# Attention norms of a six-layer transformer kernel: squares of both halves added on GpSimd, norm matmuls halved and moved

## The chip, the cores and the metric

The kernel runs on one core of one Trainium2 chip. The metric is the device time of one execution in microseconds (us). A core has engines that run side by side, each with its own queue in program order: PE (TensorE, matmuls), PEld (its weight loads), DVE (VectorE), ACT (ScalarE), POOL (GpSimd) and SP, which here only issues DMAs. Semaphores order the engines among each other.

## What is computed

A batch of 16 sequences of 256 tokens and 128 channels goes through an adaptive layer norm, a small normalised attention, and then six layers of local attention (16 heads of 64, windows of 32) with a gated feed-forward block. In each layer the queries and keys are normalised per head before the rotary turn:

```
def l2norm(t):
    return t / jnp.maximum(jnp.linalg.norm(t, axis=-1, keepdims=True), 1e-12)
...
qkv = x @ Wqkv
q, k, v = (sh(q), sh(k), sh(v))
q = l2norm(q) * qs
k = l2norm(k) * ksc
q = q * cos * scale + rotate_half(q) * sin * scale
k = k * cos * inv + rotate_half(k) * sin * inv
out = local_attention(q, k, v)
```

## The kernel before, in words

After a first part (about 165 us) the kernel walks 96 batches of work: 6 layers times 16 sequences. Each engine has an order written out by hand as a table of step names (`PE_ORDER`, `DVE_ORDER`, `ACT_ORDER`, `POOL_ORDER`, `SP_ORDER`, from line 50), and the function `walk` goes through that table once a **period**. Steps named in `AHEAD` work already on the next batch, those in `BEHIND` still on the one before, so one period holds parts of three batches. There is no scheduler: an engine runs its steps in the order of its table, and waits where a semaphore isn't there yet.

The steps that matter here; digits are the head couple p (0, 1 for k; 2, 3 for q), a token tile or a half:

- PE: `PAp`, `PBp` project the first and second halves of the head dimensions of couple p into a PSUM bank (line 1229); `NK`, `NQ` sum squares over a head with matmuls against 0/1 columns, 32 columns wide, for k and q (line 1240, eight matmuls of 256 columns, two halves into four groups of 32 rows of `small_ps`); `TK`, `TQ` transpose the clamped sums (1248); `TU` transposes the inverse k norms (1255), `KN` spreads them over the head dimensions (1264); `V0` to `V3` project values (1274); `S` are the scores (1284, 1292), `T` transpose probabilities (1303), `PV` multiply with values (1321), `WO` is the output projection (1331); `CEN` and `VAR` make the feed-forward layer norm's centring and variance (1345, 1349), `UP` and `DN` its matmuls (1360, 1367).
- DVE: `RA`, `RB` multiply a projection bank with the rotary tables (988); `CK`, `CQ` clamp the sums of squares (1016); `UC` copies the transposed inverse norms (997), `KM` scales k with them (1004); `TC` copies transposed probabilities (1033), `M` is the row maximum (1021), `XA` adds the residual into `xs1` in two instructions (1054, 1055), `XB` again into `x1` (1059), `XG` scales by the standard deviation (1064), `H` is gate times value (1071), `X` ends the layer (1076), `AR` is the reciprocal of the softmax sums (1040).
- ACT: `QA`, `QB` square a projection bank into `square` (725); `E` are the softmax exponentials, 16 heads in four parts (769); `SQ`, `LN` belong to the layer norm (777, 782, 786); `LG` and `LE` load function tables (750, 752); `G` is the gelu (793); `RTK`, `RTQ` turn sums of squares into inverse norms (742, 747); `VC` copies values, `OC` attention outputs.
- POOL: `AD` adds the two rotary products (612), `AN` scales probabilities by inverse sums (597), `RK` splits inverse k norms into three bf16 parts (583 to 591), `TB` makes the tables of the next layer, once a layer.

Before, the squares of the two halves lie in four `square` buffers; `QA2` waits until `NK` has read the k squares (`norm_made`), and `NK` waits for all four squares. The chains to keep in mind: `WO` → `XA` → `CEN` → `SQ` → `VAR` → `LN` → `XG` → `UP`, and `TU` → `UC` → `KN` → `KM` → the key move by DMA → the next period's `S`.

```
PA0 PB0 PA1 S00 S01 PB1 BI WO PA2 NK CEN PB2 VAR PA3 PB3 TK UP0 UP1 S10 S11 V0 UP2 T00 TU NQ KN0 PAD V1 PV00 KN1
TQ T01 V2 DN T10 PV01 V3 T11 PV10 PV11
```

That is the order of PE before.

Of the kernel before, what the change touches and what calls it, by code (L numbers as in the profile page):

```python
# [9 lines left out]
ALU = mybir.AluOpType  # L10
# [3 lines left out]
P = 128  # L14
BATCH, TOKENS, DIM = 16, 256, 128
DEPTH, HEADS, DIM_HEAD, WINDOW = 6, 16, 64, 32
# [12 lines left out]
QUADS = HEADS // 4  # L29
COUPLES = QUADS // 2  # L30
QK_BANKS = 4 * COUPLES
# [16 lines left out]


PE_ORDER = """  # L50
PA0 PB0 PA1 S00 S01 PB1 BI WO PA2 NK CEN PB2 VAR PA3 PB3 TK UP0 UP1 S10 S11 V0 UP2 T00 TU NQ KN0 PAD V1 PV00 KN1
TQ T01 V2 DN T10 PV01 V3 T11 PV10 PV11
"""
DVE_ORDER = """
XS RA0 RB0 RA1 M0 RB1 BI XA XB AR00 RA2 RB2 CK XG RB3 RA3 H0 M1 AR01 H1 TC00 UC H2 KM0 CQ VC1 KM1 AR10 TC01 X
AR11 TC10 VC3 TC11
"""
ACT_ORDER = """
# [1 line left out]
RTQ OC11  # L60
"""
POOL_ORDER = """
AD0 AD1 AD2 AN00 AD3 TB RK AN01 AN10 AN11
"""
SP_ORDER = """
LK MQ MK LV LL MV
# [17 lines left out]
def steps_of(text):  # L84
# [8 lines left out]
PE_ORDER, DVE_ORDER, ACT_ORDER, POOL_ORDER, SP_ORDER = (  # L93
    steps_of(text) for text in (PE_ORDER, DVE_ORDER, ACT_ORDER, POOL_ORDER, SP_ORDER))
PE_FIRST, DVE_FIRST, ACT_FIRST, POOL_FIRST = (
    [(word.split(":")[0], int(word.split(":")[1])) for word in text.split()]
    for text in (PE_FIRST, DVE_FIRST, ACT_FIRST, POOL_FIRST))
FIRST_AHEAD = max(stage for _, stage in PE_FIRST + DVE_FIRST + ACT_FIRST + POOL_FIRST)
AHEAD = ("XS", "V", "VC", "PA", "PB", "RA", "RB", "QA", "QB", "AD", "NK", "NQ", "CK", "CQ", "TK", "TQ", "RTK", "RTQ",
         "RK", "TU", "UC", "KN", "KM", "LK", "LV", "MV", "MK", "MQ", "TB")  # L100
BEHIND = ("BI", "WO", "XA", "XB", "CEN", "SQ", "VAR", "LN", "XG", "UP", "G", "H", "DN", "X", "LF", "LG")


# [5 lines left out]
def rank(order, s, *kinds):  # L109

    return [x for x in order if x[0] in kinds].index(s)
# [7 lines left out]
def build(nc, t):  # L119

    with ExitStack() as ctx:
        def sb(name, shape, dt=F32):
            return ctx.enter_context(nc.sbuf_tensor(name, shape, dt))

        def sem(name):
            return ctx.enter_context(nc.semaphore(name))
# [6 lines left out]
        norm2_ps = small_ps[:, 0:TOKENS]  # L133
# [6 lines left out]
        head_ones = sb("head_ones", [P, WINDOW])  # L140
# [24 lines left out]
        prod = sb("prod", [P, 2, 2, 2, 2 * TOKENS])  # L165
        prod_a, prod_b = ([prod[:, i, a, :, :] for i in range(2)] for a in range(2))
        square = [[sb(f"square{i}_{a}", [P, 2 * TOKENS]) for a in range(2)] for i in range(COUPLES)]
        ks = sb("ks", [P, 2, QUADS, TOKENS])
        qs = sb("qs", [P, 2, QUADS, TOKENS])
        norm2 = sb("norm2", [P, TOKENS])  # L170
# [39 lines left out]
        def carve(parts, *shape):  # L210
# [15 lines left out]
            if len(shape) == 3:  # L226
# [82 lines left out]
         f_kg, f_y, f_gw, f_xb, f_x1) = (  # L309
            sem("f_" + n) for n in ("qkv sq eps inv q2 k2 v kcol max kmax log r qfin kv kvt qt qtc kw kg y gw xb x1").split())  # L310

        xs_ready, proj_ready, prod_ready, sq_ready, rot_ready, v_made, v_even_ready, v_odd_ready = (
            sem(n) for n in ("xs_ready", "proj_ready", "prod_ready", "sq_ready", "rot_ready", "v_made",
                             "v_even_ready", "v_odd_ready"))
        norm_made, clamped, norm_turned, norms_ready, rk_parts, rk_turned, rkt_ready, kn_made, kn_ready = (
            sem(n) for n in ("norm_made", "clamped", "norm_turned", "norms_ready", "rk_parts", "rk_turned",
                             "rkt_ready", "kn_made", "kn_ready"))
# [16 lines left out]
        def at(g, per_batch, n=0):  # L334

            return g * per_batch + (CREDIT + n)

        def start_with_credit(eng, *sems):
            for s in sems:
                eng.sem_inc(s, CREDIT)  # L340
# [185 lines left out]

        @block.gpsimd
        def _(pool):
            start_with_credit(pool, scaled, rk_parts, rot_ready, f_gw, f_xb)
            pool.memset(xs[:, :], 0.0)  # L530
            pool.memset(xs1[:, :], 0.0)
            pool.memset(mean_ones[:, :], 1.0 / DIM)
# [3 lines left out]
            def make_tables(layer):  # L536
                pool.wait_ge(scales_landed, layer * 16 + 16)
                for m in range(2):
                    for a in range(2):
                        col = qk_scales[:, 2 * m + a:2 * m + a + 1]  # L540
                        pool.tensor_scalar(tables[:, m, a, a, :], rotary[:, m, 0, :], col, None, ALU.mult)
                        last = pool.tensor_scalar(tables[:, m, a, 1 - a, :], rotary[:, m, 1, :], col,
                                                  -1.0 if a else 1.0, ALU.mult, ALU.mult)
                last.then_inc(tables_ready, 1)
# [7 lines left out]
            for i in range(TILES):  # L552
                for j in range(PAIRS):
                    last = pool.tensor_copy(mask_bf[:, i, j, :], mask[:, i, :])
# [21 lines left out]
            def step(s, g, b, parity, layer):  # L576
                kind = s[0]
                if kind == "RK":

                    pool.wait_ge(norms_ready, at(g, 2, 1))  # L580
                    pool.wait_ge(rk_turned, at(g, 1))
                    alone(pool)
                    pool.tensor_copy(rk_bf[:, :, 0, :], rk[:, :, :]).then_inc(rk_parts, 1)
                    pool.wait_ge(rk_parts, at(g, 4, 1))
                    pool.tensor_tensor(rk_rest[:, :, :], rk[:, :, :], rk_bf[:, :, 0, :], ALU.subtract
                                       ).then_inc(rk_parts, 1)
                    pool.wait_ge(rk_parts, at(g, 4, 2))
                    alone(pool)
                    pool.tensor_copy(rk_bf[:, :, 1, :], rk_rest[:, :, :]).then_inc(rk_parts, 1)
                    pool.wait_ge(rk_parts, at(g, 4, 3))  # L590
                    pool.tensor_tensor(rk_bf[:, :, 2, :], rk_rest[:, :, :], rk_bf[:, :, 1, :], ALU.subtract
                                       ).then_inc(rk_parts, 1)
                if kind == "AN":
                    i, c = s[1], s[2]
                    part = slice(4 * c, 4 * c + 4)
                    pool.wait_ge(inv_ready, at(g, 2 * TILES, 2 * i + c + 1))
                    pool.tensor_tensor(probs[i][:, part, :, :].rearrange("p j e k -> p (j e) k"),  # L597
                                       probs[i][:, part, :, :].rearrange("p j e k -> p (j e) k"),
                                       inv_sums[i][:, part, :].rearrange("p j (e o) -> p (j e) o", o=1)
                                       .to_broadcast([P, PAIRS, KEYS]), ALU.mult).then_inc(scaled, 1)  # L600
                if kind == "TB" and b == BATCH - 1 and layer < DEPTH - 1:
                    pool.wait_ge(prod_ready, at(g, QK_BANKS, QK_BANKS))
                    make_tables(layer + 1)
                if kind == "AD":
                    p = s[1]
                    n, c = p // COUPLES, p % COUPLES
                    last_product = max(rank(DVE_ORDER, (h, p), "RA", "RB") for h in ("RA", "RB"))
                    pool.wait_ge(prod_ready, at(g, QK_BANKS, last_product + 1))
                    if c == 0 and g > 0:
                        pool.wait_ge((k_moved, q_moved)[n], moved(g))  # L610
                    dst = (ks, qs)[n][:, :, 2 * c:2 * c + 2, :].rearrange("p a u c -> p a (u c)")
                    pool.tensor_tensor(dst, prod_a[p % 2], prod_b[p % 2], ALU.add  # L612
                                       ).then_inc(rot_ready, 1)
# [5 lines left out]
        def _(act):  # L619
# [98 lines left out]
            def step(s, g, b, parity, layer):  # L718
                kind = s[0]
                if kind in ("QA", "QB"):  # L720
                    p, a = s[1], int(kind == "QB")
                    n = p // COUPLES
                    act.wait_ge(prod_ready, at(g, QK_BANKS, rank(DVE_ORDER, ("RB" if a else "RA", p), "RA", "RB") + 1))
                    act.wait_ge(norm_made, at(g, 2, n))
                    nc.scalar.activation(square[p % COUPLES][a][:, :], bank_of(("PB" if a else "PA", p))[:, :],  # L725
                                         ACT.Square, bias=zero_col[:, :]).then_inc(sq_ready, 1)
                if kind == "VC":
# [25 lines left out]
                if kind == "OC":  # L753
                    i, c = s[1], s[2]
# [333 lines left out]
        def _(pe):  # L1088
# [129 lines left out]
            def step(s, g, b, parity, layer):  # L1218
# [12 lines left out]
                    last.then_inc(proj_ready, 1)  # L1231
                if kind in ("NK", "NQ"):
                    n = int(kind == "NQ")
                    last_square = max(rank(ACT_ORDER, (x, COUPLES * n + c), "QA", "QB")
                                      for x in ("QA", "QB") for c in range(COUPLES))
                    pe.wait_ge(sq_ready, at(g, QK_BANKS, last_square + 1))
                    pe.wait_ge(norms_ready, at(g, 2, n))
                    for a in range(2):
                        for u in range(QUADS):
                            last = mm(norm2_ps[WINDOW * u:WINDOW * (u + 1), :], head_ones[:, :],  # L1240
                                      square[u // 2][a][:, TOKENS * (u % 2):TOKENS * (u % 2 + 1)],
                                      start=(a == 0), stop=(a == 1), skip_group_check=True)
                    last.then_inc(norm_made, 1)
                if kind in ("TK", "TQ"):
                    n = int(kind == "TQ")
# [206 lines left out]
```

## Time and profile before

| what | value |
|---|---|
| runs | 3487.27, 3490.45, 3495.57 us; median 3490.45 us |
| profiled execution | span 3500.8 us from first to last instruction (the page gives no other time for it) |
| busy | PE 96%, PEld 71%, DVE 70%, ACT 77%, POOL 41% |
| PE clock granted | mean 0.982 of full speed |
| chain that ended last | PE 69%, POOL 18%, issue 4%, DVE 2% |

The page lists busy time per engine, the chain of work that ended last, and the costliest groups of instructions by line. A timeline lists instructions in order of time with start and length; for PE the ends are modelled, so the start of one step to the start of the next is the better length of a step.

### The profile page before, as it was taken

To read this page: it belongs to the slowest core of one execution; us is meant where nothing else is said; L and a number is where in the kernel's file an instruction comes from. 1 tells how busy PE (TensorE), PEld (TensorE's weight loads), DVE (VectorE), ACT (ScalarE), POOL (GpSimd) and SP (SyncE) were. 2 spreads that over 40 slices of the span, in tenths; PEclk is the share of its full clock that TensorE was granted. 3 is DMA by queue.
4 is the path that set the end of the run, shared out by engine and by line. 5 is a ranking of instruction groups with operands and counts; after the bars stand their busy time and mean duration, and the time that the engine had idled before them with its cause. 6 is when DMAs were issued, how large, how long until landed. Compare 5 with 4: busy or idle time off the path is not lost.

```text
span 3500.8 us, 152322 instructions
## 1 busy us (share of the span) xinstructions
PE 3344.2 (96%) x63036; PEld 2479.3 (71%) x63228; DVE 2441.7 (70%) x5141; ACT 2702.7 (77%) x9033; POOL 1445.3 (41%) x1276
## 2 busy tenths in 40 slices
PE   6789999999999999999999999999999999999997
PEld 4457777677777767777767777767767767777775
DVE  5667777667777767777767777767767767777774
ACT  5667787768778777878777887868778787878876
POOL 2244444434444443444444444444444353444441
PEclk9899999999999999999999999999999999999998
DMA  2055656555655656565565566555555655565563
GB/s 71 1 115 122 140 122 129 121 123 120 143 123 123 132 118 134 127 130 126 112 138 118 127 135 131 120 130 117 127 129 121 133 129 127 117 130 126 116 135 76
DMA packets 361273, 421.42 MB, mean 120 GB/s; under 512 B 52291, under 2 KB 265814, under 8 KB 359814
## 3 DMA queue, kind: packets, MB, share of 16 engines
q1 hardware_dynamic: 360582, 411.67, 54.4%
q8 instruction: 499, 8.18, 1.0%
q14 instruction: 192, 1.57, 0.1%
HBM read 19.30 MB, written 2.10 MB: 6 GB/s over the span
## 4 chain that ended last, share of the span: by engine, by line
PE 69%; POOL 18%; issue 4%; DVE 2%; DMA 1%; ACT 1%; SPq 0%; POOLq 0%; DVEq 0%
PE ring_ps L1229 16%; POOL qs L612 12%; PE out_ps L1321 12%; PE out_ps L1331 9%; PE ring_ps L1274 8%; PE small_ps L1240 6%; PE score_ps L1292 4%; PE ring_ps L1303 4%; PE ring_ps L1367 4%; POOL probs L597 3%; DVE prod L988 2%; PE ring_ps L1264 2%; PE out_ps L1345 2%; PE score_ps L1284 1%; PE small_ps L1248 1%
## 5 line engine op out<-in xcount | busy, mean ns | idle before, releaser
L769 ACT ACTIVATE probs<-score_ps,neg_max,rq 128x64 f32<-128x64 f32 x3072 | 1194.7, 420 | 97.0 <-DVE neg_max L1026 95.7
L988 DVE TENSOR_TENSOR prod<-ring_ps,tables 128x512 f32<-128x512 f32 x1536 | 957.9, 681 | 292.4 <-PE ring_ps L1229 264.8
L612 POOL TENSOR_TENSOR ks<-prod 128x1024 f32<-128x1024 f32 x192 | 452.9, 2359 | 870.9 <-DVE prod L988 870.9
L1229 PE MATMUL ring_ps<-xs,wqk 128*128 128x256 f32 x3072 | 771.2, 389 | 17.2 <-issue 11.9
L769 ACT ACTIVATION_READ_ACCUMULATOR probs<-score_ps,neg_max,rq 128x1 f32 x3072 | 677.4, 221 | 0.0
L725 ACT ACTIVATE square<-ring_ps,biases 128x512 f32<-128x512 f32 x768 | 516.9, 687 | 200.9 <-DVE prod L988 199.1
L597 POOL TENSOR_TENSOR probs<-probs,inv_sums 128x512 f32<-128x512 f32 x384 | 401.0, 1044 | 608.8 <-DVE inv_sums L1040 608.7
L1229 PEld LDWEIGHTS ring_ps<-xs,wqk 128*128 128x128 f32 x3072 | 572.9, 192 | 107.3 <-issue 18.9
L612 POOL TENSOR_TENSOR qs<-prod 128x1024 f32<-128x1024 f32 x192 | 453.4, 2361 | 395.1 <-DVE prod L988 395.1
L1321 PEld LDWEIGHTS out_ps<-pt,v 64*64 64x64 f32 x24576 | 399.5, 136 | 119.2 <-issue 117.0
L758 ACT ACTIVATE att_t<-out_ps 128x512 f32<-128x512 f32 x384 | 217.0, 591 | 312.1 <-PE out_ps L1321 311.5
L1321 PE MATMUL out_ps<-pt,v 64*64 64x32 f32 x24576 | 433.4, 221 | 9.5 <-issue 6.7
L1274 PE MATMUL ring_ps<-wv,xs 128*128 128x512 f32 x768 | 431.1, 644 | 0.7 <-ACT vs L731 0.7
L1331 PE MATMUL out_ps<-att_t,wo 128*128 128x256 f32 x1536 | 350.9, 381 | 1.9 <-ACT att_t L758 1.2
L1292 PEld LDWEIGHTS score_ps<-kt,qt 64*32 64x32 f32 x24576 | 264.5, 105 | 90.2 <-issue 82.4
L1331 PEld LDWEIGHTS out_ps<-att_t,wo 128*128 128x128 f32 x1536 | 292.5, 191 | 43.5 <-issue 2.2
L1033 DVE COPY pt<-ring_ps 128x512 f32<-128x512 f32 x384 | 259.6, 676 | 82.2 <-PE out_ps L1321 78.2
L1292 PE MATMUL score_ps<-kt,qt 64*32 64x64 f32 x24576 | 297.8, 226 | 6.1 <-issue 5.0
L1004 DVE TENSOR_TENSOR ks<-ks,ring_ps 128x512 f32<-128x512 f32 x384 | 246.7, 684 | 73.0 <-PE ring_ps L1264 72.6
L1360 PE MATMUL out_ps<-xg,w 128*128 128x256 f32 (+1 forms) x1152 | 283.8, 383 | 3.2 <-DVE xg L1064 3.2
L1021 DVE TENSOR_REDUCE row_max<-score_ps 128x8 f32<-128x512 f32 x384 | 246.4, 684 | 24.1 <-PE score_ps L1292 20.2
L1360 PEld LDWEIGHTS out_ps<-xg,w 128*128 128x128 f32 (+1 forms) x1152 | 199.3, 180 | 80.6 <-DVE hidden L1071 30.2
(182 smaller groups left out, 3809.4 us busy)
## 6 DMA issues: line engine op xcount, KB each, us to landing
v<-vs SPq DMA_DIRECT2D x1344, 128.0 KB
qt<-qs SPq DMA_DIRECT2D x768, 128.0 KB
kt<-ks SPq DMA_DIRECT2D x768, 128.0 KB
v<-vs SPq DMA_DIRECT2D x192, 64.0 KB
wqk<-in_L_ffn_Wqkv SPq DMA_DIRECT2D x6, 1024.0 KB, 5.2
wv<-in_L_ffn_Wqkv SPq DMA_DIRECT2D x6, 512.0 KB, 4.5
wo<-in_L_ffn_Wo SPq DMA_DIRECT2D x6, 512.0 KB
out_dram<-ks SPq DMA_DIRECT2D x16, 128.0 KB, 1.9
```

Of the source, the lines that this page charges most:

```text
L597: pool.tensor_tensor(probs[i][:, part, :, :].rearrange("p j e k -> p (j e) k"), probs[i][:, part, :, :].rearrange("p j e k -> p (j e) k"), ...
L612: pool.tensor_tensor(dst, prod_a[p % 2], prod_b[p % 2], ALU.add).then_inc(rot_ready, 1)
L725: nc.scalar.activation(square[p % COUPLES][a][:, :], bank_of(("PB" if a else "PA", p))[:, :], ACT.Square, bias=zero_col[:, :]).then_inc(sq ...
L769: last = nc.scalar.activation(probs[i][:, j, e, :], score_ps[e][:, KEYS * j:KEYS * (j + 1)], ACT.Exp, bias=neg_max[:, h:h + 1], scale=rq[p ...
L988: last = V.tensor_tensor((prod_b if a else prod_a)[p % 2][:, f, :] .rearrange("p (u c) -> p u c", u=2), bank[:, :].rearrange("p (u c) -> p ...
L1033: V.tensor_copy(pt[:, 4 * c:4 * c + 4, :], bank_of(("T", i, c))[:, :].rearrange("p (j c) -> p j c", c=P)).then_inc(t_copied, 1)
L1229: last = mm(bank_of(s)[:, TOKENS * f:TOKENS * (f + 1)], wqk[:, n, 2 * c + f, a, :], xs[:, WINDOW:PADDED], start=True, stop=True)
L1274: mm(bank_of(s)[:, :], xs[:, WINDOW + P * i:WINDOW + P * (i + 1)], heads[:, :, e, :], start=True, stop=True).then_inc(v_made, 1)
L1292: last = mm(score_ps[e][WINDOW * w:WINDOW * (w + 1), KEYS * j:KEYS * (j + 1)], qt[64 * e:64 * e + 64, j, q0:q0 + WINDOW], kt[64 * e:64 * e ...
L1321: last = mm(out_ps[j % 2][side:side + 64, q0:q0 + WINDOW], v2[64 * e:64 * e + 64, WPT * i + w, DIM_HEAD * j:DIM_HEAD * (j + 1)], pt[64 * e ...
L1331: last = mm(out_ps[0][:, 0:TOKENS], wo[layer % 2][:, j, :], att_t[:, j, :], start=(j == 0), stop=(j == PAIRS - 1))
L1360: last = mm(out_ps[c % 2][0:size, TOKENS * n:TOKENS * (n + 1)], w1[layer % 2][:, col:col + size], xg[:, :], start=True, stop=True)
```

## The change

GpSimd gets a new step `SS` for each head couple p: it adds the squares of the two halves (128x512) into a buffer of their own, `square_sum`. `NK` and `NQ` then read the sums, with four matmuls in place of eight. `QAp` and `QBp` wait for the sum of the couple that used the same `square` buffers before, in place of `norm_made`. `NK` moves behind `PB2`, `NQ` from before `KN0` to behind `V2`, `TQ` from before `T01` to behind `V3`, `CQ` on DVE from between `KM0` and `VC1` to behind `TC01`.

```
 PE_ORDER = """
-PA0 PB0 PA1 S00 S01 PB1 BI WO PA2 NK CEN PB2 VAR PA3 PB3 TK UP0 UP1 S10 S11 V0 UP2 T00 TU NQ KN0 PAD V1 PV00 KN1
-TQ T01 V2 DN T10 PV01 V3 T11 PV10 PV11
+PA0 PB0 PA1 S00 S01 PB1 BI WO PA2 CEN PB2 NK VAR PA3 PB3 TK UP0 UP1 S10 S11 V0 UP2 T00 TU KN0 PAD V1 PV00 KN1
+T01 V2 NQ DN T10 PV01 V3 TQ T11 PV10 PV11
 """
 DVE_ORDER = """
-XS RA0 RB0 RA1 M0 RB1 BI XA XB AR00 RA2 RB2 CK XG RB3 RA3 H0 M1 AR01 H1 TC00 UC H2 KM0 CQ VC1 KM1 AR10 TC01 X
+XS RA0 RB0 RA1 M0 RB1 BI XA XB AR00 RA2 RB2 CK XG RB3 RA3 H0 M1 AR01 H1 TC00 UC H2 KM0 VC1 KM1 AR10 TC01 CQ X
 AR11 TC10 VC3 TC11
 """
...
 POOL_ORDER = """
-AD0 AD1 AD2 AN00 AD3 TB RK AN01 AN10 AN11
+AD0 SS0 AD1 SS1 AD2 AN00 AD3 TB RK AN01 SS2 SS3 AN10 AN11
 """
...
+        square_sum = [sb(f"square_sum{i}", [P, 2 * TOKENS]) for i in range(COUPLES)]
...
+                if kind == "SS":
+                    p = s[1]
+                    n, c = p // COUPLES, p % COUPLES
+                    last_square = max(rank(ACT_ORDER, (x, p), "QA", "QB") for x in ("QA", "QB"))
+                    pool.wait_ge(sq_ready, at(g, QK_BANKS, last_square + 1))
+                    pool.wait_ge(norm_made, at(g, 2, n))
+                    pool.tensor_tensor(square_sum[c][:, :], square[c][0][:, :], square[c][1][:, :], ALU.add
+                                       ).then_inc(sum_ready, 1)
...
-                    act.wait_ge(norm_made, at(g, 2, n))
+                    act.wait_ge(sum_ready, at(g, 2 * COUPLES, p - 1))
...
                 if kind in ("NK", "NQ"):
                     n = int(kind == "NQ")
-                    last_square = max(rank(ACT_ORDER, (x, COUPLES * n + c), "QA", "QB")
-                                      for x in ("QA", "QB") for c in range(COUPLES))
-                    pe.wait_ge(sq_ready, at(g, QK_BANKS, last_square + 1))
+                    pe.wait_ge(sum_ready, at(g, 2 * COUPLES, COUPLES * (n + 1)))
                     pe.wait_ge(norms_ready, at(g, 2, n))
-                    for a in range(2):
-                        for u in range(QUADS):
-                            last = mm(norm2_ps[WINDOW * u:WINDOW * (u + 1), :], head_ones[:, :],
-                                      square[u // 2][a][:, TOKENS * (u % 2):TOKENS * (u % 2 + 1)],
-                                      start=(a == 0), stop=(a == 1), skip_group_check=True)
+                    for u in range(QUADS):
+                        last = mm(norm2_ps[WINDOW * u:WINDOW * (u + 1), :], head_ones[:, :],
+                                  square_sum[u // 2][:, TOKENS * (u % 2):TOKENS * (u % 2 + 1)],
+                                  start=True, stop=True, skip_group_check=True)
                     last.then_inc(norm_made, 1)
```

Line numbers of the changed kernel are 1 to 9 higher than those before. What the tables make of the queues, first on PE in the middle of a period, from `WO` to `VAR`, before:

```order
L1331 MATMUL out_ps<-att_t,wo 128x256 x8
L1229 MATMUL ring_ps<-xs,wqk 128x256 x2
L1240 MATMUL small_ps<-square_0,head_ones 32x256 x4
L1240 MATMUL small_ps<-square_1,head_ones 32x256 x4
L1345 MATMUL out_ps<-xs,center 128x256
L1229 MATMUL ring_ps<-xs,wqk 128x256 x2
L1349 MATMUL out_ps<-xc_sq,mean_ones 128x256
```

and the same stretch now:

```order
L1337 MATMUL out_ps<-att_t,wo 128x256 x8
L1238 MATMUL ring_ps<-xs,wqk 128x256 x2
L1351 MATMUL out_ps<-xs,center 128x256
L1238 MATMUL ring_ps<-xs,wqk 128x256 x2
L1246 MATMUL small_ps<-square_sum,head_ones 32x256 x4
L1355 MATMUL out_ps<-xc_sq,mean_ones 128x256
```

`CEN` now follows `PA2` at once, and `NK` with half its matmuls stands between `PB2` and `VAR`. Then on PE from `TU` to `T11` in the second half of a period, before:

```order
L1255 MATMUL ring_ps<-ident_bf,rk_bf 48x128 x2
L1240 MATMUL small_ps<-square_0,head_ones 32x256 x4
L1240 MATMUL small_ps<-square_1,head_ones 32x256 x4
L1264 MATMUL ring_ps<-rkt,head_sel_bf 128x256 x2
L1274 MATMUL ring_ps<-wv,xs 128x512
L1321 MATMUL out_ps<-pt,v 64x32 x32
L1264 MATMUL ring_ps<-rkt,head_sel_bf 128x256 x2
L1248 MATMUL small_ps<-ident,norm 128x128 x2
L1303 MATMUL ring_ps<-ident,probs 128x128 x4
L1274 MATMUL ring_ps<-wv,xs 128x512
L1367 MATMUL ring_ps<-hidden,w_1 128x256 x3
```

and now:

```order
L1261 MATMUL ring_ps<-ident_bf,rk_bf 48x128 x2
L1270 MATMUL ring_ps<-rkt,head_sel_bf 128x256 x2
L1280 MATMUL ring_ps<-wv,xs 128x512
L1327 MATMUL out_ps<-pt,v 64x32 x32
L1270 MATMUL ring_ps<-rkt,head_sel_bf 128x256 x2
L1309 MATMUL ring_ps<-ident,probs 128x128 x4
L1280 MATMUL ring_ps<-wv,xs 128x512
L1246 MATMUL small_ps<-square_sum,head_ones 32x256 x4
L1373 MATMUL ring_ps<-hidden,w_1 128x256 x3
```

`KN0`, which reads what `UC` copies out of `TU`'s bank, now stands directly behind `TU`; `NQ` stands between `V2` and `DN`, and `TQ` (1248, now 1254) left this stretch for the place between `V3` and `T11`. Last on POOL, one period now:

```order
L621 TENSOR_TENSOR ks<-prod 128x2x512
L611 TENSOR_TENSOR square_sum<-square_0,square_1 128x512
L621 TENSOR_TENSOR ks<-prod 128x2x512
L611 TENSOR_TENSOR square_sum<-square_0,square_1 128x512
L621 TENSOR_TENSOR qs<-prod 128x2x512
L598 TENSOR_TENSOR probs<-probs,inv_sums 128x512
```

Before, the two `ks` adds and the `qs` add follow each other with nothing between them; the other two sums stand behind the second `probs` step of the period.

## Rows read from the trace of the kernel before

**Rows 1.** The page: the span, and the chain that ended last by engine.

```profile
span 3500.8 us, 152322 instructions
...
PE 69%; POOL 18%; issue 4%; DVE 2%; DMA 1%; ACT 1%; SPq 0%; POOLq 0%; DVEq 0%
```

**Rows 2.** The tile `square`: duration ns min/median/max of one, first and last start.

```profile
L1240 PE MATMUL small_ps<-square,head_ones x3072: 379/379/636, 174.4 to 3424.2; 128*32 128x256 f32 x192
```

**Rows 3.** Busy time by engine in the stretch of one period, `S00` to `S00`.

```profile
1699.47:1732.74 33.27, 33.12 (x650) 24.84 (x652) 23.65 (x48) 26.71 (x90) 14.39 (x12) 1.00 0.56 119
```

**Rows 4.** Timeline of PE in that period: start us, length us, line, tiles, shapes, count.

```profile
1705.70 1.03 PE L1229 MATMUL ring_ps<-xs,wqk 128*128 128x256 f32 x4
1706.66 1.07 PE L1240 MATMUL small_ps<-square,head_ones 128*32 128x256 f32 x16
1707.66 0.70 PE L1345 MATMUL out_ps<-xs,center 128*128 128x256 f32 x2
1708.20 1.03 PE L1229 MATMUL ring_ps<-xs,wqk 128*128 128x256 f32 x4
1709.06 0.59 PE L1349 MATMUL out_ps<-xc_sq,mean_ones 128*128 128x256 f32 x2
1709.49 1.89 PE L1229 MATMUL ring_ps<-xs,wqk 128*128 128x256 f32 x8
...
1717.58 0.29 PE L1255 MATMUL ring_ps<-ident_bf,rk_bf 128*48 128x128 bf16 x2
1717.80 1.07 PE L1240 MATMUL small_ps<-square,head_ones 128*32 128x256 f32 x16
1718.81 0.39 PE L1264 MATMUL ring_ps<-rkt,head_sel_bf 48*128 48x256 bf16 x2
...
1722.28 1.02 PE L1274 MATMUL ring_ps<-wv,xs 128*128 128x512 f32 x2
1723.14 1.46 PE L1367 MATMUL ring_ps<-hidden,w 128*128 128x256 f32 x6
...
1727.00 0.60 PE L1303 MATMUL ring_ps<-ident,probs 128*128 128x128 f32 x4
```

**Rows 5.** Timeline of ACT in that period.

```profile
1708.15 0.25 ACT L769 ACTIVATION_READ_ACCUMULATOR probs<-score_ps,neg_max,rq 128x1 f32 x1
1708.40 0.47 ACT L777 ACTIVATE xc_sq<-out_ps,biases 128x256 f32<-128x256 f32 x1
...
1714.67 0.47 ACT L793 ACTIVATE gate<-out_ps,b_full 128x256 f32<-128x256 f32 x1
...
1724.95 0.26 ACT L769 ACTIVATION_READ_ACCUMULATOR probs<-score_ps,neg_max,rq 128x1 f32 x1
```

**Rows 6.** Timeline of DVE in that period.

```profile
1706.34 0.43 DVE L1055 TENSOR_TENSOR xs<-out_ps,x_all 64x255 f32<-64x255 f32 x1
...
1707.24 1.24 DVE L988 TENSOR_TENSOR prod<-ring_ps,tables 128x512 f32<-128x512 f32 x2
...
1711.42 2.49 DVE L988 TENSOR_TENSOR prod<-ring_ps,tables 128x512 f32<-128x512 f32 x4
1715.18 0.48 DVE L1071 SCALAR_TENSOR_TENSOR hidden<-out_ps,b_full,gate 128x256 f32<-128x256 f32 x1 [1.28 <-ACT gate L793]
...
1718.18 0.27 DVE L997 COPY rkt<-ring_ps 48x256 bf16<-48x256 bf16 x1
```

**Rows 7.** Timeline of POOL in that period; in brackets the idle time before it.

```profile
1704.32 2.36 POOL L612 TENSOR_TENSOR ks<-prod 128x1024 f32<-128x1024 f32 x1 [2.45 <-DVE prod L988]
1710.63 2.36 POOL L612 TENSOR_TENSOR qs<-prod 128x1024 f32<-128x1024 f32 x1 [3.95 <-DVE prod L988]
...
1723.16 1.04 POOL L597 TENSOR_TENSOR probs<-probs,inv_sums 128x512 f32<-128x512 f32 x1 [4.62 <-DVE inv_sums L1040]
1725.53 1.04 POOL L597 TENSOR_TENSOR probs<-probs,inv_sums 128x512 f32<-128x512 f32 x1 [1.33 <-DVE inv_sums L1040]
```

**Rows 8.** Waits of PE: what waited for what, us in total, times, longest.

```profile
PE ring_ps L1255 <- POOL rk_bf L591: 37.1, 9, 6.3
```

More of the change, by code:

```diff
@@ L99 @@
 AHEAD = ("XS", "V", "VC", "PA", "PB", "RA", "RB", "QA", "QB", "AD", "NK", "NQ", "CK", "CQ", "TK", "TQ", "RTK", "RTQ",
-         "RK", "TU", "UC", "KN", "KM", "LK", "LV", "MV", "MK", "MQ", "TB")
+         "SS", "RK", "TU", "UC", "KN", "KM", "LK", "LV", "MV", "MK", "MQ", "TB")
 BEHIND = ("BI", "WO", "XA", "XB", "CEN", "SQ", "VAR", "LN", "XG", "UP", "G", "H", "DN", "X", "LF", "LG")
@@ L310, in build @@
             sem("f_" + n) for n in ("qkv sq eps inv q2 k2 v kcol max kmax log r qfin kv kvt qt qtc kw kg y gw xb x1").split())
-        xs_ready, proj_ready, prod_ready, sq_ready, rot_ready, v_made, v_even_ready, v_odd_ready = (
-            sem(n) for n in ("xs_ready", "proj_ready", "prod_ready", "sq_ready", "rot_ready", "v_made",
+        xs_ready, proj_ready, prod_ready, sq_ready, sum_ready, rot_ready, v_made, v_even_ready, v_odd_ready = (
+            sem(n) for n in ("xs_ready", "proj_ready", "prod_ready", "sq_ready", "sum_ready", "rot_ready", "v_made",
                              "v_even_ready", "v_odd_ready"))
@@ L528, in _ @@
         def _(pool):
-            start_with_credit(pool, scaled, rk_parts, rot_ready, f_gw, f_xb)
+            start_with_credit(pool, scaled, rk_parts, rot_ready, sum_ready, f_gw, f_xb)
             pool.memset(xs[:, :], 0.0)
```

## The prediction, made before the changed kernel ran

> **What bounds the kernel now.** I read the page first: the chain that ended last lies on PE for 69% and on POOL for 18% of a span of 3500.8 us [rows 1]. Then I looked for the period. The norm matmuls are issued 3072 times, the first at 174.4 and the last at 3424.2 us [rows 2]; the first `NK` and the last `NQ` are 95 periods and the 11.1 us between `NK` and `NQ` [rows 4] apart, so a period takes (3424.2 - 174.4 - 11.1) / 95 = 34.1 us on average. An ordinary one, `S00` to `S00`, takes 33.27 us, and PE is busy in 33.12 of them, ACT in 26.71, DVE in 23.65, POOL in 14.39, with PE's clock granted in full, at 2.4 GHz [rows 3]. The rest of the average is the change of layer, where `TU` waits for POOL up to 6.3 us [rows 8], and single longer periods. So PE is full, and a matmul less seems a gain. But PE may be full because its steps were fitted into each other's waits. The question is what stands in the holes once `NK` and `NQ` leave them. The timelines of one period answer that: PE [rows 4], ACT [rows 5], DVE [rows 6], POOL [rows 7].
>
> **What is removed.** `NQ` takes 1717.80 to 1718.81 = 1.01 us, `NK` 1.00 us [rows 4]. Its 16 records last 1.07 us from first start to last end and one lasts 0.379 [rows 2, 4], so four waves of four start (1.07 - 0.38) / 3 = 0.23 us apart. Without two waves, 1.01 - 2 x 0.23 = 0.55 us is left; half of all would be 0.50. Both steps together save 0.9 us a period, 95 x 0.9 = 86 us in all, if nothing takes their place.
>
> **What is added on POOL.** Four adds of 128x512. An add of 128x1024 takes 2.36 us, the `probs` step of 128x512 with a small second operand 1.04 [rows 7]; so one takes 1.04 to 1.4 us, and I take 1.18, half of the larger, since it reads two full operands like it. `SS0` fits into the 2.45 us before the second `ks` add, `SS1` into the 3.95 us before the first `qs` add, `SS2` and `SS3` into the 4.62 us before `AN10` [rows 7]: 4.7 us a period in gaps, at no cost. `SS1` ends at 1704.32 + 2.36 + 1.18 = 1707.86 and `SS3` at 1723.16 - 4.62 + 2.36 = 1720.9; both are done before their new readers start (below). `QA` and `QB` wait for sums made long before; `CQ` now waits on DVE with `X` and `AR11` behind it, but `X` waits for `DN`, which comes after `NQ`, and `AR11` for exponentials that end at 1725.21 [rows 5]; no cost. `TQ` is whole as before, only elsewhere on PE: nothing gained or lost.
>
> **First place, PA2 to VAR.** Before: `PA2` 0.96, `NK` 1.00, `CEN` 0.54, `PB2` 0.86, and `VAR` starts at 1709.06 [rows 4]. `CEN` reads `xs1`, whose second part ends on DVE at 1706.34 + 0.43 = 1706.77 [rows 6]; `NK` ran in that wait. Hand-overs take about 0.05 us: the gelu ends at 1715.14 and `H0` starts at 1715.18 [rows 5, 6]. So `CEN` now starts no earlier than 1706.82, 0.2 us after `PA2` leaves PE free. Steps beside a 32-column step are longer: `PA2` before `NK` takes 0.96 where `PB2` takes 0.86; `CEN` behind it 0.54 where `VAR` takes 0.43 (1709.06 to 1709.49) [rows 4]. New sum: 1706.82 + `CEN` 0.54 + `PB2` 0.96 + `NK` 0.55 = 1708.87, and `VAR` starts 0.19 us earlier. `SQ`, which `VAR` waits for, can't help more: it stands behind exponentials that end at 1708.40, and ends itself at 1708.87 [rows 5], so `VAR` can't start before 1708.92. Behind `NK`, `VAR` is longer by 0.11. What follows comes 0 to 0.19 us earlier; I take 0.15 out of the 0.45 saved.
>
> **Second place, TU to T11.** Before, `NQ` ran between `TU` and `KN0`. `KN0` needs `UC`, which ends at 1718.18 + 0.27 = 1718.45 [rows 6]. `UC` stands in DVE's queue behind `H0`, `M1`, `AR01`, `H1`, `TC00`, back to back from 1715.18, when the gelu of `G0` lets `H0` go [rows 5, 6]; and `G0` follows from `LN` through ACT's queue without a gap. So `UC` moves only by what `VAR` moves, 0.15: `KN0` at 1718.45 - 0.15 + 0.05 = 1718.35 in place of 1718.81, 0.46 earlier, and not the 1.01 that `NQ` took [rows 4]. PE stands still for over half a microsecond there: **the removed step was a filler**. Further on `NQ` comes back between `V2` and `DN`, where PE never waited: 0.55, plus 0.10 for `V2` before it (0.86 so far, 1722.28 to 1723.14 [rows 4]) and 0.11 for `DN` behind it: 0.76. `T11` comes at 1727.00 - 0.46 + 0.76 = 1727.30, **0.30 us later**. From `T11` on, PE runs through to the next `S01`, whose maximum starts the exponentials that lead to `SQ`, `LN` and `G0`: the delay returns every period.
>
> The 0.21 us for the neighbours of `NQ` come from the rows of `NK`'s neighbours. The Trainium skill, TensorEngine Tiling (Array Packing), Tiling Modes, says that a change of tiling mode, not of tile alone, drains the engine. By that rule the new place costs what `NK`'s place does, and the sum stays; without it `T11` would be 0.09 us late and the kernel at 3499 us.
>
> **Sum.** In the five changes of layer `UC` runs at once behind `TU`: `TU` 0.22, `UC` 0.27 and two hand-overs make 0.59 to `KN0` in place of 1.23, and 0.76 come back, 0.12 more, while POOL reaches `RK` some 0.15 earlier because the third product is ready sooner: nothing. The other 90 periods pay 0.30 us: 27 us. The sum is against the profiled execution, 3500.8 us, which would become 3528; that one lies 10 us above the median of the runs, 3490.45, and the same difference gives **3517.5 us**. The forecast's bounds: with a shift of 0.19, half a step (0.50) and no dearer neighbours `T11` moves by 0; with no shift and all of 0.76 by +0.45. That is 3490 to 3531.
>
> **Rivals.**
> *PE's work decides after all (faster).* If `UC` can come early enough, PE closes the hole: `KN0` at 1717.80, and `T11` earlier by 1.01 - 0.76 + 0.15 = 0.40. Another wait ends this at about the same place: `T11` needs `AN11`, which ends at 1725.53 + 1.04 = 1726.57 [rows 7], so it gains 0.38 at most: 95 x 0.38 = 36 us, 3454. It decides once `UC` ends before 1717.75, 0.7 us earlier than now. For it: PE's 33.12 of 33.27 us [rows 3]. Against it: the gapless chain from `LN` to `UC`.
> *The two cancel (no change).* If the neighbours of `NQ` cost nothing there and `VAR` gains 0.19: 3490 to 3497.
> *The adds hold up DVE (slower still).* Each can block DVE for at most its own 1.18 us where PE waits for DVE, 95 x 1.18 = 112 us, 3602. Against it: with POOL idle DVE makes two products in 1.24 us, with POOL adding beside it four in 2.49 [rows 6, 7], the same. The Trainium skill, SBUF — State Buffer, states that the port pair of VectorE and GpSimd is locked by a VectorE instruction with two SBUF inputs, or in a two-port mode, against a GpSimd one that reads SBUF. By that rule nothing is blocked, since the products, clamps and copies beside the new adds take at most one operand from SBUF; the trace agrees, with 0.62 us for a product either way.
>
> **How the numbers follow.** A measurement of this kernel tells 0.2%, 7 us, from no change. My forecast has 0.66; within its bounds of 3490 to 3531 about one part in eight is under 3497. PE's work decides: 0.21. The two cancel: 0.10. The adds hold up DVE: 0.03. Slower by over 7 us: 0.58 + 0.03 = 0.61; within 7 us 0.08 + 0.10 = 0.18; faster 0.21. The likeliest case's own range is 3490 to 3531; the whole reaches down to 3468, which takes in the faster case where only a part of its 36 us comes, and up to 3534.
>
> **What would show it.** In the profile after, `NK` and `NQ` should be groups of about 0.6 us with 8 records; PE should show a wait for `UC` (DVE `rkt`) before `KN0` of 0.5 to 0.6 us nearly every period, and one for `xs1` before `CEN` of 0.1 to 0.3; PE's busy share should fall by 2 to 3 points; the time from `KN0` to `T11` should grow from 8.19 us to about 8.95, and an ordinary period from 33.1 to about 33.4. POOL should show four adds near 1.18 us and a busy share near 54%. It is wrong if `KN0` follows `TU` without a wait, if `KN0` to `T11` stays near 8.7, or if an ordinary period is under 33.0.

## The result and the profile after

The changed kernel takes 3583.6 us (median of 4 runs, 3576.04 to 3584.8); the kernel before, measured beside it, 3493.01 us (3487.27 to 3498.58). The ratio is 1.0259 (95% interval 1.0243 to 1.0275): some 90 us slower, where 27 were forecast and 3534 was the upper end of the range. The direction was right, the size was not.

The page of the profile after (span, engines, the chain that ended last, the new group on POOL):

```profile
span 3581.1 us, 150019 instructions
...
PE 3312.7 (93%) x61500; PEld 2415.8 (67%) x61692; DVE 2535.0 (71%) x5141; ACT 2692.0 (75%) x9033; POOL 1915.9 (53%) x1660
...
PE 67%; ACT 13%; DVE 9%; issue 8%; POOL 2%; DMA 1%; SPq 0%; DVEq 0%; POOLq 0%; ACTq 0%
...
L611 POOL TENSOR_TENSOR square_sum<-square,square 128x512 f32<-128x512 f32 x384 | 483.9, 1270 | 0.0
```

The 384 adds are there, 1.27 us each, and POOL's share is 53%. What was not forecast is in the chain: before it lay on PE and POOL and hardly on ACT and DVE (1% and 2%) [rows 1]; now ACT holds 13% of it and DVE 9%. So something ahead of ACT is late, and ACT's exponentials wait for one thing on DVE, `neg_max` of step `M`. Its group in the list by line (busy us, mean ns | the engine's idle time before it, and what ended that), with the exponentials that wait for it, first before, then after:

```profile
L1026 DVE SCALAR_TENSOR_TENSOR neg_max<-row_max,rq 128x16 f32<-128x16 f32 x192 | 35.1, 183 | 6.7
...
L769 ACT ACTIVATE probs<-score_ps,neg_max,rq 128x64 f32<-128x64 f32 x3072 | 1194.7, 420 | 97.0 <-DVE neg_max L1026 95.7
```

```profile
L1035 DVE SCALAR_TENSOR_TENSOR neg_max<-row_max,rq 128x16 f32<-128x16 f32 x192 | 114.2, 595 | 6.7
...
L778 ACT ACTIVATE probs<-score_ps,neg_max,rq 128x64 f32<-128x64 f32 x3072 | 1193.6, 422 | 179.3 <-DVE neg_max L1035 178.1
```

Same instruction, same shape, 79 us more, and ACT waits 82 us longer for it. The timelines of one period after, DVE (start, length):

```profile
1707.18 1.29 DVE L1030 TENSOR_REDUCE row_max<-score_ps 128x8 f32<-128x512 f32 x2
1708.51 1.21 DVE L1035 SCALAR_TENSOR_TENSOR neg_max<-row_max,rq 128x16 f32<-128x16 f32 x1
...
1723.43 0.18 DVE L1035 SCALAR_TENSOR_TENSOR neg_max<-row_max,rq 128x16 f32<-128x16 f32 x1
```

and POOL:

```profile
1706.10 2.36 POOL L621 TENSOR_TENSOR ks<-prod 128x1024 f32<-128x1024 f32 x1 [7.12 <-DVE prod L997]
1708.40 1.27 POOL L611 TENSOR_TENSOR square_sum<-square,square 128x512 f32<-128x512 f32 x1
```

`M1`'s `neg_max`, which starts while POOL runs nothing, takes 0.18 us. `M0`'s starts 0.11 us after `SS0` and ends at 1709.72, 0.05 us after `SS0` ends (1708.40 + 1.27 = 1709.67): it lasts until the add is over. `M0`'s takes over half a microsecond in 88 of the 96 periods. In ACT's queue `QB1`, which `SS1` and so `NK` need, and `SQ`, which `VAR` needs, stand behind the first exponentials. What that does on PE, in the same period:

```profile
1705.27 0.38 PE L1290 MATMUL score_ps<-mask_bf,ident_bf 128*128 128x512 bf16 x1
...
1714.62 0.64 PE L1246 MATMUL small_ps<-square_sum,head_ones 128*32 128x256 f32 x8 [0.45 <-POOL square_sum L611]
1715.49 0.70 PE L1355 MATMUL out_ps<-xc_sq,mean_ones 128*128 128x256 f32 x2 [0.23 <-ACT xc_sq L786]
...
1725.04 0.39 PE L1270 MATMUL ring_ps<-rkt,head_sel_bf 48*128 48x256 bf16 x2 [0.64 <-DVE rkt L1006]
...
1734.00 0.60 PE L1309 MATMUL ring_ps<-ident,probs 128*128 128x128 f32 x4
...
1739.43 0.38 PE L1290 MATMUL score_ps<-mask_bf,ident_bf 128*128 128x512 bf16 x1
```

An ordinary period now takes 1739.43 - 1705.27 = 34.16 us. Three waits stand in it: 0.45 ahead of `NK`, 0.23 ahead of `VAR`, 0.64 ahead of `KN0`. Only the last was forecast. Over the whole run the first two add up to 59.3 us (us in total, times, longest):

```profile
PE small_ps L1246 <- POOL square_sum L611: 39.7, 79, 4.6
PE out_ps L1355 <- ACT xc_sq L786: 19.6, 80, 1.6
```

For comparison, an ordinary period of before (`S00`, `KN0`, `T11`, `S00`):

```profile
1529.35 0.38 PE L1284 MATMUL score_ps<-mask_bf,ident_bf 128*128 128x512 bf16 x1
...
1548.71 0.39 PE L1264 MATMUL ring_ps<-rkt,head_sel_bf 48*128 48x256 bf16 x2
...
1556.90 0.60 PE L1303 MATMUL ring_ps<-ident,probs 128*128 128x128 f32 x4
...
1562.42 0.38 PE L1284 MATMUL score_ps<-mask_bf,ident_bf 128*128 128x512 bf16 x1
```

It takes 33.07, so between these two the change costs 1.09 us. The period shown of before is one of the shorter ones: over all 95 the median is 33.22 us before and 34.17 now, 0.95 more, and 95 x 0.95 gives the 90 us. In the two shown, `S00` to `KN0` takes 19.77 in place of 19.36 (+0.41), `KN0` to `T11` 8.96 in place of 8.19 (+0.77, forecast +0.76), and `T11` to `S00` 5.43 in place of 5.52. The forecast had the first of the three as 0.46 *less*.

### The profile page after: what moved, and what is told of

It is laid out like the page before. It is cut to its first block, busy times and chain, and to the rows that moved or that the text cites. A ratio compares the mean times of both kernels' runs of the same rounds, so it can differ in the third digit from the quotient of the medians.

```text
span 3581.1 us, 150019 instructions
## 1 busy us (share of the span) xinstructions
PE 3312.7 (93%) x61500; PEld 2415.8 (67%) x61692; DVE 2535.0 (71%) x5141; ACT 2692.0 (75%) x9033; POOL 1915.9 (53%) x1660
## 4 chain that ended last, share of the span: by engine, by line
PE 67%; ACT 13%; DVE 9%; issue 8%; POOL 2%; DMA 1%; SPq 0%; DVEq 0%; POOLq 0%; ACTq 0%
PE ring_ps L1238 12%; PE out_ps L1327 11%; PE ring_ps L1280 11%; ACT probs L778 10%; PE score_ps L1298 7%; PE out_ps L1366 6%; PE ring_ps L1309 5%; PE ring_ps L1373 4%; DVE neg_max L1035 2%; PE ring_ps L1270 2%; DVE row_max L1030 2%; PE out_ps L1355 2%; PE small_ps L1246 2%; PE score_ps L1290 2%; DVE prod L997 2%
## 5 line engine op out<-in xcount | busy, mean ns | idle before, releaser
L997 DVE TENSOR_TENSOR prod<-ring_ps,tables 128x512 f32<-128x512 f32 x1536 | 949.5, 680 | 220.8 <-PE ring_ps L1238 206.5
L778 ACT ACTIVATION_READ_ACCUMULATOR probs<-score_ps,neg_max,rq 128x1 f32 x3072 | 686.5, 223 | 0.0
L611 POOL TENSOR_TENSOR square_sum<-square,square 128x512 f32<-128x512 f32 x384 | 483.9, 1270 | 0.0
L1327 PEld LDWEIGHTS out_ps<-pt,v 64*64 64x64 f32 x24576 | 392.2, 136 | 118.5 <-issue 116.5
L1327 PE MATMUL out_ps<-pt,v 64*64 64x32 f32 x24576 | 426.1, 221 | 9.5 <-issue 7.5
```

Of the source, the lines that this page charges most:

```text
L611: pool.tensor_tensor(square_sum[c][:, :], square[c][0][:, :], square[c][1][:, :], ALU.add).then_inc(sum_ready, 1)
L778: last = nc.scalar.activation(probs[i][:, j, e, :], score_ps[e][:, KEYS * j:KEYS * (j + 1)], ACT.Exp, bias=neg_max[:, h:h + 1], scale=rq[p ...
L997: last = V.tensor_tensor((prod_b if a else prod_a)[p % 2][:, f, :] .rearrange("p (u c) -> p u c", u=2), bank[:, :].rearrange("p (u c) -> p ...
L1327: last = mm(out_ps[j % 2][side:side + 64, q0:q0 + WINDOW], v2[64 * e:64 * e + 64, WPT * i + w, DIM_HEAD * j:DIM_HEAD * (j + 1)], pt[64 * e ...
```

## The experiments

**Theory A:** `SS0` beside `M0` holds DVE's `neg_max`; that is most of the 90 us, and what is left is the forecast's emptied hole. **Theory B:** the hole and the matmuls' new places cost it all, and `neg_max` is late because everything is. **Theory C:** POOL's added work as such (its queue longer by four adds) is what delays. Each ratio below is against the kernel before, measured beside it: 3488.03 us for `e1` to `e4`, 3490.15 us for `e5` to `e8`.

### e1: `SS0` waits until `M0` is done

```diff
+                    if p == 0 and g > 0:
+                        pool.wait_ge(nb_ready, at(g - 1, TILES, 1))
                     pool.tensor_tensor(square_sum[c][:, :], ...
```

> The changed kernel, and the first add SS0 also waits until the M0 scaling of the maxima (neg_max) of the same period is done, so that the two no longer run at the same time. Theory A (the first add holds up neg_max, 1.03 us in place of 0.17, and with it the exponentials): neg_max is back at 0.17 us and the kernel at 3500 to 3530 us, where the prediction had it. Rival B (the new places of NK and NQ on PE cost three times what was forecast, and neg_max is long only in time that is idle anyway): 3560 to 3590 us, as the changed kernel.

3523.5 us, ratio 1.0099 (1.0082 to 1.0116). DVE and POOL of one period:

```profile
1686.71 0.17 DVE L1037 SCALAR_TENSOR_TENSOR neg_max<-row_max,rq 128x16 f32<-128x16 f32 x1
```

```profile
1687.06 1.27 POOL L613 TENSOR_TENSOR square_sum<-square,square 128x512 f32<-128x512 f32 x1 [0.54 <-DVE neg_max L1037]
```

and PE:

```profile
1683.33 0.38 PE L1292 MATMUL score_ps<-mask_bf,ident_bf 128*128 128x512 bf16 x1
...
1690.69 0.70 PE L1353 MATMUL out_ps<-xs,center 128*128 128x256 f32 x2
...
1692.18 0.64 PE L1248 MATMUL small_ps<-square_sum,head_ones 128*32 128x256 f32 x8
...
1701.37 0.29 PE L1263 MATMUL ring_ps<-ident_bf,rk_bf 128*48 128x128 bf16 x2
1702.30 0.39 PE L1272 MATMUL ring_ps<-rkt,head_sel_bf 48*128 48x256 bf16 x2 [0.63 <-DVE rkt L1008]
...
1711.26 0.60 PE L1311 MATMUL ring_ps<-ident,probs 128*128 128x128 f32 x4
...
1716.69 0.38 PE L1292 MATMUL score_ps<-mask_bf,ident_bf 128*128 128x512 bf16 x1
```

The waits ahead of `NK` and `VAR` are gone, in this period and but for two each in the whole run:

```profile
PE small_ps L1248 <- POOL square_sum L613: 7.9, 2, 4.1
PE out_ps L1357 <- ACT xc_sq L788: 2.0, 2, 1.4
```

That is 49 us less than in the changed kernel, and all four adds are still made: C falls. The ordinary period is 33.36, 0.29 over before (0.30 by the medians, 33.52 and 33.22), where 0.30 was forecast; `KN0` follows `TU` with 0.63 us of nothing, and `KN0` to `T11` takes 8.96 (forecast 8.95). So this kernel is the one that was forecast, and with it 55 of the 90 us fall away: B falls for those.

### e2: the kernel before with `SS0` alone

```diff
-AD0 AD1 AD2 AN00 AD3 TB RK AN01 AN10 AN11
+AD0 SS0 AD1 AD2 AN00 AD3 TB RK AN01 AN10 AN11
...
+                if kind == "SS":
...
+                    pool.wait_ge(sq_ready, at(g, QK_BANKS, last_square + 1))
+                    pool.tensor_tensor(square_sum[0][:, :], square[0][0][:, :], square[0][1][:, :], ALU.add
+                                       ).then_inc(sum_ready, 1)
...
+                    if p == 2:
+                        act.wait_ge(sum_ready, at(g, 1, 1))
```

> The kernel before, with SS0 alone added on GpSimd behind the first rotary add; its sum is read by nothing, all norm matmuls stay as and where they were. Theory A: neg_max takes 1.0 us in nearly every period and the kernel 3560 to 3590 us, 0.8 to 0.9 us a period more. Rival B: no more than 3500 us.

3550.23 us, ratio 1.0174 (1.0155 to 1.0193). The sum is read by nothing; PE does exactly the work of before, in the old order, and the kernel still loses 62 us. DVE and POOL:

```profile
1683.92 1.17 DVE L1035 SCALAR_TENSOR_TENSOR neg_max<-row_max,rq 128x16 f32<-128x16 f32 x1
```

```profile
1683.79 1.27 POOL L609 TENSOR_TENSOR square_sum<-square,square 128x512 f32<-128x512 f32 x1
```

The two end within 0.03 us of each other again; `neg_max` takes over half a microsecond in 92 of 96 periods. A stands by itself, without a change on PE. The time lies below the 3560 to 3590 that were expected: `M0`'s `neg_max` is 0.87 us longer on average, and 62 us are 0.65 us a period. Why the rest does not reach the kernel's time was not followed.

### e3: `M0` reads its row maxima from PSUM

```diff
+                    maxima = row_max[:, :, :]
+                    if i == 0:
+                        dve.wait_ge(o_copied, at(g, 2 * TILES))
+                        maxima = out_ps[1][:, 480:496].rearrange("p (j e) -> p j e", e=2)
...
-                        last = V.tensor_reduce(row_max[:, :, e],
+                        last = V.tensor_reduce(maxima[:, :, e],
...
```

This is the changed kernel, with `SS0` where the change put it and one operand of `neg_max` in a free corner of a PSUM bank (and one wait on PE, so that `BI` does not overwrite it).

> The changed kernel, the row maxima of tile 0 written to a free piece of PSUM in place of SBUF, so that neg_max of M0 has one operand in SBUF and not two; SS0 stays where it is, beside it. Theory A with its cause in the two SBUF operands: neg_max at about 0.2 us beside the add, 3500 to 3530 us. Rival C (the add holds DVE up in another way, by its place in time or its semaphores, whatever the operands): neg_max stays at 1.0 us and the kernel at 3570 to 3590 us.

3530.73 us, ratio 1.0113 (1.0096 to 1.013), much as `e1` and 0.7 us above the expected range. DVE and POOL:

```profile
3074.22 0.17 DVE L1039 SCALAR_TENSOR_TENSOR neg_max<-out_ps,rq 128x16 f32<-128x16 f32 x1
```

```profile
3073.95 1.27 POOL L611 TENSOR_TENSOR square_sum<-square,square 128x512 f32<-128x512 f32 x1
```

`neg_max` now runs and ends in the middle of the add, in 86 of 96 periods, and never takes more than 0.18 us. So it is not the time at which it runs nor its semaphores (the rival C of this expectation): it is the second operand in SBUF.

### e8: `SS0` of e2 as a memset

```diff
-                    pool.tensor_tensor(square_sum[0][:, :], square[0][0][:, :], square[0][1][:, :], ALU.add
-                                       ).then_inc(sum_ready, 1)
+                    pool.memset(square_sum[0][:, :], 0.0).then_inc(sum_ready, 1)
```

The buffer is 1280 columns wide here, so that it lasts about as long as the add; nothing reads it.

> As e2_only_ss0, with a memset of 128x1280 in place of the add: GpSimd is busy at the same place for a like time, but reads nothing from SBUF. If neg_max is held because GpSimd reads SBUF beside it: neg_max at 0.17 us and 3485 to 3500 us. If any GpSimd instruction at that place holds it: neg_max near the memset's end and above 3530 us.

3490.53 us, ratio 0.9996 (0.9979 to 1.0013). DVE and POOL:

```profile
1520.80 0.18 DVE L1034 SCALAR_TENSOR_TENSOR neg_max<-row_max,rq 128x16 f32<-128x16 f32 x1
```

```profile
1520.68 1.17 POOL L609 MEMSET square_sum<- 128x1280 f32 x1
```

Same place, same waits, 1.17 us of POOL around the whole of `neg_max` in 95 of 96 periods, no cost. The memset only writes: what holds DVE is that POOL *reads* SBUF.

### e4, e5, e7: the hole between `TU` and `KN0` filled

In `e4` (on `e3`) and `e5` (on `e1`) `V1` goes into the hole (`PAD` issues no work, it only holds a place in the ring of banks), its copy `VC1` on DVE ahead of `KM0`, and `TQ` goes ahead of `V3`:

```diff
-PA0 PB0 PA1 S00 ... T00 TU KN0 PAD V1 PV00 KN1
-T01 V2 NQ DN T10 PV01 V3 TQ T11 PV10 PV11
+PA0 PB0 PA1 S00 ... T00 TU V1 PAD KN0 PV00 KN1
+T01 V2 NQ DN T10 PV01 TQ V3 T11 PV10 PV11
...
-... H2 KM0 VC1 KM1 AR10 TC01 CQ X
+... H2 VC1 KM0 KM1 AR10 TC01 CQ X
```

`e7` is `e5` with `TQ` left behind `V3`.

> As e3_max_in_psum, and V1 moves on PE into the hole between TU and KN0, its copy on DVE ahead of KM0, and TQ ahead of V3. If the hole at KN0 is what the halved norms lose, as the prediction has it: KN0 follows V1 with hardly a wait, T11 comes some 0.3 us earlier than before, and the kernel takes 3450 to 3480 us, faster than both. If the hole costs nothing: the time of e3_max_in_psum.

> SS0 waits as in e1_ss0_waits, and PE and DVE have the order of e4_fill (V1 in the hole behind TU, TQ ahead of V3). The wait does what the maxima in PSUM did there: an ordinary period of 32.7 us and 3462 to 3476 us. If the wait of SS0 costs something that PSUM did not: above 3476 us.

> As e1_ss0_waits, and V1 alone moves into the hole behind TU (its copy ahead of KM0); TQ stays behind V3. If V1 closes the hole, KN0 to T11 loses V1's 1.05 us and the hole is used: 0.3 to 0.6 us a period less than e1_ss0_waits, 3470 to 3495 us; V3 then waits for the last value copy on ACT, so that a part is lost again, and it stays slower than e5_wait_and_fill by about 0.2 us a period.

`e4`: 3473.97 us, 0.9955 (0.9941 to 0.997). `e5`: 3466.73 us, 0.9922 (0.9908 to 0.9936). `e7`: 3468.88 us, 0.9934 (0.9921 to 0.9946). PE of `e5`:

```profile
1617.16 0.59 PE L1292 MATMUL score_ps<-mask_bf,ident_bf 128*128 128x512 bf16 x2
...
1635.39 0.29 PE L1263 MATMUL ring_ps<-ident_bf,rk_bf 128*48 128x128 bf16 x2
1635.61 1.12 PE L1282 MATMUL ring_ps<-wv,xs 128*128 128x512 f32 x2
1636.67 0.39 PE L1272 MATMUL ring_ps<-rkt,head_sel_bf 48*128 48x256 bf16 x2
...
1649.83 0.59 PE L1292 MATMUL score_ps<-mask_bf,ident_bf 128*128 128x512 bf16 x2
```

`V1` covers the wait for `UC`, `KN0` follows without idle time, and the period is 32.67 where `e1` had 33.36 (medians 32.81 and 33.52). From `e1` to `e5` that is 57 us, and as much from `e3` to `e4`, which were measured beside the same kernel before; `e5` is faster than both kernels. `V1` alone brings 55 of it (`e7`, just under its expected range). The place of `TQ` stays open: `e7` was expected 0.2 us a period slower than `e5`, but the two differ by less than their intervals tell.

### e6: the order of e5 with whole norms

No adds; `NK` and `NQ` with eight matmuls each, and squares of `q` in buffers of their own. Here the matmuls against those of `e5`:

```diff
-                    for u in range(QUADS):
-                        last = mm(norm2_ps[...], head_ones[:, :], square_sum[u // 2][...],
-                                  start=True, stop=True, ...)
+                    for a in range(2):
+                        for u in range(QUADS):
+                            last = mm(norm2_ps[...], head_ones[:, :], square[COUPLES * n + u // 2][a][...],
+                                      start=(a == 0), stop=(a == 1), ...)
```

> The order of e5_wait_and_fill without the adds: NK and NQ at their new places with eight matmuls on eight squares (q has square buffers of its own), no SS. If halving the matmuls is worth 0.46 us at each place once the holes are filled: 0.5 to 0.9 us a period more than e5_wait_and_fill, 3510 to 3555 us. If the gain over the kernel before came from the new order of V1 and TQ alone: the time of e5_wait_and_fill.

3528.16 us, ratio 1.0098 (1.0081 to 1.0115). Its norms on PE:

```profile
1134.44 1.07 PE L1240 MATMUL small_ps<-square,head_ones 128*32 128x256 f32 x16
...
1148.50 1.07 PE L1240 MATMUL small_ps<-square,head_ones 128*32 128x256 f32 x16
```

With the same order of steps, half the norm matmuls, with the adds that they need, are worth 3528.16 - 3466.73 = 61 us; the new order alone, with whole norms, is 3528.16 - 3490.15 = 38 us slower than before. The gain that the change was after exists; the order in which the change put it did not let it through.

## Why the prediction was wrong in size

**The failed step** is the term that put the adds at nothing, "4.7 us a period in gaps, at no cost", with the sentence that backed it among the rivals: "nothing is blocked, since the products, clamps and copies beside the new adds take at most one operand from SBUF". That list of DVE's instructions was not complete. `M0`'s `neg_max` reads `row_max` and `rq`, both in SBUF, and it stands just behind the place where `SS0` went. The rival "the adds hold up DVE" named the right mechanism with a chance of 0.03. It was sized as at most 1.18 us a period, 112 us; `neg_max` lasts about 1.0 us in place of 0.17, in 88 of 96 periods, and that costs 3583.6 - 3523.5 = 60 us against `e1`, or 56 once each is set against its own measurement of before (1.0259 - 1.0099 = 1.6%). So about 35 of the 90 us are what was forecast, and the rest is this term.

The Trainium skill, SBUF — State Buffer, Who interferes with whom, says that a VectorE instruction with two SBUF inputs contends with a GpSimd instruction that reads SBUF, not with one that only writes it; one with at most one SBUF input, outside the two-port modes, does not contend. The Trainium skill, SBUF — State Buffer, Summary: rules for kernel authors, adds that the second of the two to issue blocks fully until the first is done. The runs agree: 1.17 us beside an add, up to the add's end (`e2`), 0.17 with one input in PSUM (`e3`), 0.18 beside a memset (`e8`). As far as it bears on an add, the prediction read the rule rightly; it applied it to the long instructions and not to the small one on the critical chain.

The trace of before showed it already, in its first period. The tile `neg_max`, then the row of the longest one, and POOL's beside it:

```profile
L1026 DVE SCALAR_TENSOR_TENSOR neg_max<-row_max,rq x192: 174/175/1273, 204.4 to 3455.6; 128x16 f32<-128x16 f32 x192
```

```profile
215.52 1.27 DVE L1026 SCALAR_TENSOR_TENSOR neg_max<-row_max,rq 128x16 f32<-128x16 f32 x1
```

```profile
214.41 2.35 POOL L612 TENSOR_TENSOR qs<-prod 128x1024 f32<-128x1024 f32 x1
```

The median is 175 ns and the longest 1273, ending with an add of POOL (214.41 + 2.35 = 216.76, 215.52 + 1.27 = 216.79). In an ordinary period of before the add that precedes `SS0` was nearly in the way as well:

```profile
1532.79 0.18 DVE L1026 SCALAR_TENSOR_TENSOR neg_max<-row_max,rq 128x16 f32<-128x16 f32 x1
```

```profile
1530.18 2.36 POOL L612 TENSOR_TENSOR ks<-prod 128x1024 f32<-128x1024 f32 x1 [6.77 <-DVE prod L988]
```

It ends at 1532.54, a quarter of a microsecond before `neg_max` starts. The gap on POOL was real, but DVE's instruction stood right behind its beginning.

**Confirmed, point by point** (on `e1`, where the collision is taken away):
- `NK` and `NQ` shrink from 1.07 us with 16 records [rows 4] to 0.64 with 8. `NK` to the start of `VAR` is 0.57; forecast 0.55.
- `CEN` waits for `xs1`. In the waits of the changed kernel PE's weight loads for it stand in 96 periods, 0.5 us on average:

```profile
PEld out_ps L1351 <- DVE xs L1064: 48.4, 96, 1.3
```

  PE itself loses less, since part of that wait lies beside `PA2`: `CEN` of `e1` starts 1690.69 - 1689.58 = 1.11 us after `PA2` does, and the forecast had 1706.82 - 1705.70 = 1.12. Taking 0.96 for `PA2`, as before, 0.15 of it is waiting; taking the 0.86 of `PB2`, 0.25.
- `NQ` was a filler: 0.63 us of hole ahead of `KN0`, "over half a microsecond" forecast. Filling it gave 55 us back with `V1` alone (`e7`), 57 with `TQ` moved too (`e5`).
- `NQ` between `V2` and `DN` costs 0.77, against 0.76; the ordinary period grows by 0.29, against 0.30. The neighbours are dearer as forecast: `V2` takes 0.96 in place of 0.86, `DN` 1.40 in place of 1.30, and `VAR` behind `NK` 0.54 in place of 0.43. One of the rows read for this was no evidence: `CEN` takes 0.54 in `e1` too, where no 32-column step stands beside it.
- The forecast's sum was 27 us, `e1` measures 3523.5 - 3488.03 = 35 (29 to 40 by its interval). The ordinary periods account for 90 x 0.29 = 26; where the other few microseconds lie was not tried.

**A small miss without effect:** an add of 128x512 takes 1.27 us, not 1.18; inside the bounds of 1.04 to 1.4.

**"PE's work decides after all"** (0.21) did not come: it asked for an earlier `UC`. `e5` came near its number (0.78% faster, where 36 us would be 1.0%) in another way, by giving the hole new work.

## What to carry to other kernels

Before new work is put into an idle stretch of GpSimd, list every VectorE instruction that runs beside it with its operands' memories, the shortest too: one of 0.17 us that heads ACT's chain cost some 60 us here. A longest duration of seven times the median was the sign, already in the trace of before, that it can be held. When a step leaves its place, ask which wait it was covering, and give that place another step that is ready; here the same halved norms lost 35 us with the hole open and won 23 with it filled (`e1`, `e5`). If the two would meet, one operand in PSUM (`e3`) or one wait on the less urgent engine (`e1`) takes the collision away.

## What was not expected of the hardware

The add sets how long the hold lasts: an instruction of 16 elements a partition waits for an add of 512, up to its end (1709.72 against 1709.67, and 1685.09 against 1685.06 in `e2`). In the changed kernel the two meet in 90 periods, and in 89 of these `neg_max` ends within 0.05 us of the add's end. Held instructions of other sizes were not tried. And DVE's products, which read one operand from PSUM and one from SBUF, took no longer beside 384 more adds (1536 of them are busy for 949.5 us in all, 957.9 before), so two reading engines alone are not enough: in every run here, what was held had both of DVE's operands in SBUF and a reading instruction on POOL beside it.
